# A four-layer graph transformer on one core: two bias rows fetched later, expert offsets in fp16, column sums on ScalarE, half a Gram matrix

## What is computed

```python
# layer 0 mixer, twice: ... h = gelu(y @ W1 + b1); stream += h @ W2 + b2
# layer 0 experts (8, two chosen per node):
combine = chosen_weights                        # 1250 x 8
x = x + sum_e combine[:, e] * (relu(y @ w1[e] + b1[e]) @ w2[e] + b2[e]) + shared
# layer 3 mixer:
XW_v, theta_X = X @ W_v.T, X @ W_theta.T
first = mean(XW_v, axis=nodes)                  # = mean(X) @ W_v.T
kv = theta_X.T @ XW_v                           # = W_theta (X.T X) W_v.T
x = x + first + X @ kv / (n * sqrt(d))
```

## Time and profile before

| | |
|---|---|
| median of 3 runs | 3285.67 us (3276.35 to 3289.95) |
| profiled execution | 3295.35 us, of which the span is 3293.6 us |
| busy, share of the span | PE 85%, DVE 51%, POOL 36%, ACT 32% |
| mean granted clock of PE | 0.91 |
| DMA | 415.33 MB, mean 126 GB/s |

### The profile page before, as it was taken

The page is one execution under the profiler, slowest core; times in us unless marked ns, Lnnn a source line. Parts: engine busy times, 40 slices in busy tenths (PEclk is TensorE's granted clock), DMA queues, the critical chain, the costliest instruction groups (busy, mean ns, idle before and its releaser), DMA issues. The chain is left out here.

```text
span 3293.6 us, 45745 instructions
## 1 busy us (share of the span) xinstructions
PE 2804.8 (85%) x16779; PEld 1790.3 (54%) x16779; DVE 1675.3 (51%) x3399; ACT 1067.9 (32%) x2432; POOL 1182.0 (36%) x1445
## 2 busy tenths in 40 slices
PE   8997899869999986989997893999879968669874
PEld 4654567535556754555554562777535646445553
DVE  8765667523556762266643536222245456552543
ACT  3243436312432642122321431444332315320132
POOL 2031677638367763863312122111103306400042
PEclk9998989889998988998998896999989979888887
DMA  2001445324144531451100001999820039710098
GB/s 61 1 26 58 124 148 163 103 67 128 36 119 143 159 118 48 128 138 34 41 19 26 13 26 53 412 417 416 332 53 30 33 114 325 244 42 0 32 342 270
DMA packets 163939, 415.33 MB, mean 126 GB/s; under 512 B 23931, under 2 KB 75675, under 8 KB 140236
## 3 DMA queue, kind: packets, MB, share of 16 engines
q1 hardware_dynamic: 149213, 362.10, 32.4%
q0 software_dynamic: 12960, 42.48, 3.4%
q10 hardware_dynamic: 1555, 7.95, 1.0%
HBM read 325.37 MB, written 87.09 MB: 125 GB/s over the span
## 5 line engine op out<-in xcount | busy, mean ns | idle before, releaser
L2587 POOL TENSOR_SCALAR raw<-raw 128x512 f32<-128x512 f32 x380 | 261.9, 689 | 1219.9 <-PE ps L492 300.8
L506 PE MATMUL ps<-units,ARENA 128*125 128x512 f16 x2160 | 479.2, 384 | 56.8 <-POOL units L2591 56.2
L506 PEld LDWEIGHTS ps<-units,ARENA 128*125 128x125 f16 x2160 | 292.8, 138 | 238.7 <-POOL units L2591 56.8
L1751 DVE TENSOR_TENSOR ARENA<-tmp,ARENA 128x500 f16<-128x500 f32 (+3 forms) x289 | 198.4, 690 | 399.2 <-ACT ARENA L1326 215.9
L492 PE MATMUL ps<-ARENA,units 128*128 128x500 f16 (+1 forms) x2160 | 389.0, 342 | 2.0 <-DVE ARENA L2476 2.0
L492 PEld LDWEIGHTS ps<-ARENA,units 128*128 128x128 f16 x2160 | 211.5, 98 | 179.3 <-issue 7.8
L1325 ACT ACTIVATE tmp<-ps,cols 128x500 f32<-128x500 f32 (+1 forms) x204 | 129.7, 636 | 443.1 <-PE ps L492 402.4
L2591 POOL TENSOR_TENSOR AT<-raw,AT 128x512 f16<-128x512 f32 x200 | 235.9, 1179 | 17.0
L2591 POOL TENSOR_TENSOR units<-raw,units 128x512 f16<-128x512 f32 x180 | 220.0, 1222 | 15.3
L2635 POOL DMA_INDIRECT ARENA<-rows_d,proj x81 | 80.3, 991 | 389.0 <-DVE ARENA L2106 363.0
L2640 POOL DMA_INDIRECT picks_d<-ARENA,proj x81 | 81.9, 1011 | 347.4 <-DVE ARENA L2146 346.7
(11 more groups left out here) (439 smaller groups left out, 4856.7 us busy)
## 6 DMA issues: line engine op xcount, KB each, us to landing
ARENA<-split_d SPq DMA_DIRECT2D x135, 1024.0 KB
raw<-in_moe SPq DMA_DIRECT2D x200, 256.0 KB, 3.0
split_d<-AT SPq DMA_DIRECT2D x200, 256.0 KB, 2.5
raw<-in_units SPq DMA_DIRECT2D x180, 256.0 KB, 2.5
ARENA<-split_d SPq DMA_DIRECT2D x27, 1280.0 KB
rows_d<-ARENA SPq DMA_DIRECT2D x6, 896.0 KB
ARENA<-picks_d SPq DMA_DIRECT2D x6, 896.0 KB
ARENA<-picks_d ACTq DMA_DIRECT2D x6, 896.0 KB
```

What stands on the lines that cost most here:

```text
L506: ins = pe.matmul(o[0:R, :], th(srcT, h, k, t, 1), w(k, g), start=(i == 0), stop=(i == len(steps) - 1))
L1751: tt(lo, tmp[:, staged[0] % STAGES, 0:width], hi, ALU.subtract).then_inc(sem("lo_T"), s.one("lo_T"))
L2587: pool.tensor_scalar(r, r, WEIGHT_SCALE, 1.0, ALU.mult, ALU.mult).then_inc(sem("pool_step"), 1)
```

## The change

It has four parts. The note of the place for b20 and b21 is taken in block 1 of the MLP, with its second unit, instead of block 0 with its first. The expert offsets are one fp16 product on 72 rows: rows 0 to 7 hold the high part of the combination weights with the high part of the biases, rows 32 to 39 the weights' low part with the high part, rows 64 to 71 the high part with the biases' low part; the rest is zero. DVE prepares the biases (`bias_parts`, between the low parts) and the weights (in `gates`), and E0's slot is freed there. The column sums of layer 3 come from the accumulator output of ACT's evictions of M's transposes, and DVE adds the three chunks. Of the Gram matrix PE computes for block k only the columns from 128 k on; the blocks below the diagonal are transposed from those above (`gram_below`), and ACT evicts them to their places.

```diff
@@ -198,7 +198,10 @@
-        combT = K[0:NE, N:2 * N]
+        combT = K[0:72, N:N + N // 2].bitcast(F16)
+        comb_parts = K[0:R, 2000:2000 + T * 72].rearrange("p (t e) -> p t e", e=72)
+        comb_hi = K[0:R, 2720:2720 + T * NE // 2].bitcast(F16).rearrange("p (t e) -> p t e", e=NE)
+        bias_rows16 = K[0:72, 2800:2800 + D // 2].bitcast(F16)
         comb3 = comb[0:R, :].rearrange("p (t e) -> p t e", e=NE)
@@ -237,6 +240,7 @@
+        column_sums = stats[:, :, 0:1].rearrange("p (k c) a -> p k (c a)", k=KC)
@@ -780,7 +784,6 @@
                     if b == 0:
-                        uses_row()
                         by_chunks(lambda c: transposed_chunk(lambda t, a, b: nat(Y, t, a, b), "y", "yT", c),
@@ -788,6 +791,8 @@
                     u, w = unit()
+                    if b == 1:
+                        uses_row()
                     gemm_N("Q", lambda k, g: w[:, g, k, :], "read_dve", by_chunk=True, waits=(0, KC, KC) if b == 0 else (KC, KC, KC))
@@ -847,14 +852,13 @@
                     for j in range(nt):
-                        ins = pe.transpose(o[0:8, j * R:(j + 1) * R], comb3[:, t0 + j, :], ident[0:R, 0:R])
+                        ins = pe.transpose(o[0:72, j * R:(j + 1) * R], comb_parts[:, t0 + j, :], ident[0:R, 0:R])
                     ins.then_inc(sem("filled_act"), 1)
                 pe.wait_ge(sem("combT"), s.more("combT", 3))
-                pe.wait_ge(sem(f"row_loaded{ROWS.index(row) % ROW_SLOTS}"), 16 * (ROWS.index(row) // ROW_SLOTS + 1))
                 for t in range(T):
...
                     o = bank("dve", "read_dve")
-                    pe.matmul(o[0:R, :], combT[:, t * R:(t + 1) * R], row_slots[0:8, ROWS.index(row) % ROW_SLOTS, :], start=True, stop=True).then_inc(sem("filled_dve"), 1)
+                    pe.matmul(o[0:R, :], combT[:, t * R:(t + 1) * R], bias_rows16, start=True, stop=True).then_inc(sem("filled_dve"), 1)
@@ -1247,19 +1251,29 @@
-            for k in range(KC):
+            def gram_rows(k):
                 pe.wait_ge(*left("act"))
...
                 for t in range(T):
-                    ins = pe.matmul(o[:, :], nat(M, t, k * 128, (k + 1) * 128), nat(M, t), start=(t == 0), stop=(t == T - 1))
+                    ins = pe.matmul(o[:, k * 128:D], nat(M, t, k * 128, (k + 1) * 128), nat(M, t, k * 128, D), start=(t == 0), stop=(t == T - 1))
                 ins.then_inc(sem("filled_act"), 1)
-            pe.wait_ge(*left("dve"))
-            o = bank("dve", "read_dve")
-            for k in range(KC):
-                for t in range(T):
-                    ins = pe.matmul(o[:, k:k + 1], nat(M, t, k * 128, (k + 1) * 128), ones[0:R, 0:1], start=(t == 0), stop=(t == T - 1))
-            ins.then_inc(sem("filled_dve"), 1)
-            pe.wait_ge(sem("G"), s.more("G", KC))
+
+            def gram_below(k):
+                pe.wait_ge(sem("G"), s.more("G", 2 if k == 2 else 1))
+                pe.wait_ge(*left("act"))
+                o = bank("act", "G")
+                for j in range(k + 1, KC):
+                    ins = pe.transpose(o[:, j * 128:(j + 1) * 128], G[:, k * D + j * 128:k * D + (j + 1) * 128], ident[:, :])
+                ins.then_inc(sem("filled_act"), 1)
+
+            gram_rows(0)
+            gram_rows(1)
+            gram_below(0)
+            gram_rows(2)
+            gram_below(1)
+            gram_rows(3)
+            gram_below(2)
+            pe.wait_ge(sem("G"), s.more("G", KC - 1))
             pe.wait_ge(*loaded(True))
@@ -1327,13 +1341,14 @@
-            def evac_direct(dst, order="c", groups=None):
+            def evac_direct(dst, order="c", groups=None, sums=None):
...
                     direct_banks.append(o)
-                    act.activation(th(dst, 0, k, t0, nt), o[:, 0:nt * R], ACT.Identity).then_inc(sem("hi_D"), s.one("hi_D"))
+                    act.activation(th(dst, 0, k, t0, nt), o[:, 0:nt * R], ACT.Identity,
+                                   accum_out=sums(k, t0 // CH[0][1]) if sums else None).then_inc(sem("hi_D"), s.one("hi_D"))
@@ -1576,7 +1591,7 @@
                 for t0, nt in CH:
-                    evac("act", "combT", combT[:, t0 * R:(t0 + nt) * R], nt * R, p=8)
+                    evac("act", "combT", combT[:, t0 * R:(t0 + nt) * R], nt * R, p=72)
@@ -1688,10 +1703,26 @@
-            by_chunks(lambda c: evac_direct("YT", groups=(KC * c, KC * c + KC)), high_chunk)
+            by_chunks(lambda c: evac_direct("YT", groups=(KC * c, KC * c + KC), sums=lambda k, c: column_sums[:, k, c:c + 1]), high_chunk)
             evac("both", "x_sel", x_sel[0], D, p=SEL)
-            for k in range(KC):
-                evac("act", "G", G[:, k * D:(k + 1) * D], D)
+            def gram_rows(k):
+                act.wait_ge(sem("filled_act"), s.more("filled_act"))
+                o = s.bank("act")
+                act.activation(G[:, k * D + k * 128:(k + 1) * D], o[:, k * 128:D], ACT.Identity).then_inc(sem("G"), s.one("G"))
+
+            def gram_below(k):
+                act.wait_ge(sem("filled_act"), s.more("filled_act"))
+                o = s.bank("act")
+                act.activation(G[:, (k + 1) * D:].rearrange("p (j c) -> p j c", c=D)[:, :, k * 128:(k + 1) * 128],
+                               o[:, (k + 1) * 128:D].rearrange("p (j c) -> p j c", c=128), ACT.Identity).then_inc(sem("G"), s.one("G"))
+
+            gram_rows(0)
+            gram_rows(1)
+            gram_below(0)
+            gram_rows(2)
+            gram_below(1)
+            gram_rows(3)
+            gram_below(2)
             for k in range(KC):
@@ -2287,8 +2318,26 @@
                     step(tt(w1, w1, lg, ALU.mult))
-                    step(tt(comb3, w1, bc(mr), ALU.mult), "comb")
-                    step(ts(combs[0:R, :], comb[0:R, :], WS, None, ALU.mult))
+                    step(tt(comb3, w1, bc(mr), ALU.mult))
+                    ts(combs[0:R, :], comb[0:R, :], WS, None, ALU.mult)
+                    step(dve.tensor_copy(comb_hi, comb3))
+                    dve.tensor_copy(comb_parts[:, :, 0:8], comb_hi)
+                    dve.tensor_copy(comb_parts[:, :, 64:72], comb_hi)
+                    step(tt(comb_parts[:, :, 32:40], comb3, comb_hi, ALU.subtract), "comb")
+
+            def bias_parts(name):
+
+                j = ROWS.index(name)
+                dve.wait_ge(sem(f"row_loaded{j % ROW_SLOTS}"), 16 * (j // ROW_SLOTS + 1))
+                slot = row_slots[0:72, j % ROW_SLOTS, :]
+                dve.memset(comb_parts, 0.0)
+                ts(slot, slot, WEIGHT_SCALE, None, ALU.mult).then_inc(sem("dve_step"), s.one("dve_step"))
+                dve.wait_ge(*s.latest())
+                dve.tensor_copy(bias_rows16, slot).then_inc(sem("dve_step"), s.one("dve_step"))
+                dve.wait_ge(*s.latest())
+                tt(bias_rows16[64:72, :], slot[64:72, :], bias_rows16[64:72, :], ALU.subtract).then_inc(sem("dve_step"), s.one("dve_step"))
+                dve.wait_ge(*s.latest())
+                row_free(name)
@@ -2300,12 +2349,12 @@
             low_parts("Q", "hT", 0)
+            bias_parts("E0")
             low_direct("YT", (8, 12))
...
             low_parts("Q", "hT", 2)
-            add_to(X, "read_dve", scale=1.0)
-            row_free("E0")
+            add_to(X, "read_dve")
             for e in range(NE):
@@ -2515,9 +2564,9 @@
-            dve.wait_ge(sem("filled_dve"), s.more("filled_dve"))
-            o = s.bank("dve")
-            ts(colsT[:, 0:4], o[:, 0:4], 1.0 / N, None, ALU.mult).then_inc(sem("read_dve"), s.one("read_dve"))
+            dve.tensor_reduce(colsT[:, 4:8], column_sums, AX_X, ALU.add).then_inc(sem("dve_step"), s.one("dve_step"))
+            dve.wait_ge(*s.latest())
+            ts(colsT[:, 0:4], colsT[:, 4:8], 1.0 / N, None, ALU.mult).then_inc(sem("dve_step"), s.one("dve_step"))
             dve.wait_ge(*s.latest())
@@ -2700,7 +2749,7 @@
                 if name[0] == "E":
-                    sp.dma_start(slot[0:40, :], eb_in[int(name[1])]).then_inc(sem(f"row_loaded{j % ROW_SLOTS}"), 16)
+                    sp.dma_start(slot[0:72, :], eb_in[int(name[1])]).then_inc(sem(f"row_loaded{j % ROW_SLOTS}"), 16)
                 elif name == "gb2":
@@ -2877,9 +2926,9 @@
     rows = np.stack([r[n] for n in VEC_ROWS])
-    eb = np.zeros((4, 40, D), np.float32)
+    eb = np.zeros((4, 72, D), np.float32)
     for i, rows_of in enumerate((a["L0_ffn_b2"], a["L1_ffn_be2"], np.concatenate([a["L2_ffn_n1"], a["L2_ffn_n2"]], 1), a["L3_ffn_b2"])):
-        eb[i, 0:NE] = eb[i, 32:32 + NE] = rows_of
+        eb[i, 0:NE] = eb[i, 32:32 + NE] = eb[i, 64:64 + NE] = rows_of
     proj = a["L0_mix_proj"].transpose(0, 2, 1)
```

## The result

| | kernel before | changed kernel |
|---|---|---|
| median | 3281.01 us (4 runs, 3273.92 to 3289.95) | 3197.10 us (4 runs, 3192.38 to 3201.46) |
| profiled execution | 3295.35 us, span 3293.6 | 3192.38 us, span 3190.6 |
| mean granted clock | 0.910 | 0.926 |

The ratio is 0.9743, with a 95% interval of 0.9711 to 0.9774: 84 us, where 96 were forecast. The two profiled executions lie 103 us apart. Neither number is the gain: the profiled execution of before took longer than each of its four runs, that of after is the fastest of its own, and the experiments show what they differ in besides the change. In one later series one execution (offsets_early_again, 3426.54 us at a granted clock of 0.825) was in a slower state of the chip, and its median is given without it.

What follows compares the result with a forecast made beforehand. TensorE was taken as the bound, with time lost to its idle gaps, extra work and low clock. Terms 60.6 + 8.0 + 25.7 + 2.2 - 0.4 = 96.1 us, taken from 3285.67, gave 3190 us, range 3172 to 3222.

Steps and rivals of the forecast that it cites:

- The row's place: Second MLP block's W2, layer 0: later bias row load removes 56.2 us idle and 4.3 us low clock, together 60.6 us.
- to spare: Second block's W2: POOL has its weights split at 686, PE wants them at 701.0, leaving 15 us.
- The offsets: Layer 0's expert bias product: faster products less DVE's added work win 8 us, bounds 6.6 to 10.5.
- The ten products: Experts' offset matmuls: paced by DVE's evictions, they take 5.7 us where L857 holds PE 16.36 us.
- DVE's four instructions: Between hT's low parts and the last direct low parts: 2.35 us, 2.45 with waits, all on the path.
- Column sums and Gram matrix: Layer 3: the stretch falls from 49.35 to 23.6 us, 25.7 won; the W_v product behind it wins 2.2.
- The end wait: Before the product with W_v: the last two evictions follow each other on ACT, about 1.1 us, bounds 0.6 and 1.6.
- the accumulator's reads: ACT's twelve evictions of layer 3's transposes: 211 ns each, 0.4 us lost, bounds 0 and 2.5.
- POOL as the bound in block 2: Rival, second MLP block: DVE's row addition slows POOL, PE stands 30 us in all, 3220 us; chance 0.07.
- The queue standing: Rival: SP's queue also waits at the row's new place, 28 us lost twice, 3250 us; chance 0.03.
- The clock down in the Gram stretch: Rival, layer 3: clock stays low from 384 columns on, 7.4 us become 15, 2.2 stay lost, 3200 us; chance 0.09.
- Slower by a late E0 row: Rival, experts: DVE waits for E0's row, each us late costing one; above 3302 needs 112 us; chance 0.01.

Runs made afterwards that it cites:

- offsets_early_again: Second series of the changed kernel with DVE's four new instructions one call earlier, before the low parts of hT's first chunk; 3198.97 us against the changed kernel's 3192.43.
- the run with one unit: Kernel before with only the bias row's load one unit later instead of three; 3233.35 us, ratio 0.9836 to the kernel before.
- offsets_early: Changed kernel with DVE's four new instructions one call earlier, before the low parts of hT's first chunk; first series 3189.48 us against the changed kernel's 3204.39.
- three_memsets: Changed kernel with three more DVE memsets of 600 columns between its memset and the scaling of E0's row; 3202.05 us in one run.

## Why the prediction was right, and where not

- **The total.** Forecast 96.1 us. The changed kernel was compared with the one before three times: 83.9, 92.4 and 101.2 us by the medians, 92.5 in the mean (the ratios, 0.9743, 0.9728 and 0.9703, stand for 84, 90 and 98). The forecast of 3190 us lies 7 under the first median; the range 3172 to 3222 held it. The timelines give 60.9 + 6.6 + 28.6 = 96.1 us, the very sum that was forecast. That is luck in the last digit: the terms were off by +0.3, -1.4 and +1.1 us, which cancel.
- **The row's place**, 60.6: measured 60.9 in the timeline. Both halves (56.2 of idle time, 4.3 of low clock behind it) went whole: no gap is left, and W2 takes 26.06 us both times. The chain from DVE's tenth addition over SP and POOL to PE was the right one, as the run with one unit shows. POOL had 12.8 us to spare, not 15.
- **The offsets**, 8: this is the step that was mis-sized; the runs have 6.6. The ten products came as forecast (5.49 for 5.7), DVE's four instructions too (2.15 for 2.45, up to 3.27 beside GpSimd). But the 16.36 us that they replace was read from one execution, and the mean over six is 15.2: 1.1 us less. I costed DVE's delay as its own length, where PE's wait grew by 1.9 to 3.4 us (2.6 in the mean) depending on what GpSimd did to DVE at that moment. And a term was missing: the 48 gate products behind that wait took 5.1 us in each of the five traces with the new offsets in the old order, all at the low clock, and 3.2 to 5.1, mean 4.3, in the six with the old ones. The W2 behind the offsets gave back 0.7 us (28.9 to 28.2), and some 0.5 lie in smaller pieces.
- **Column sums and Gram matrix**, 25.7 + 2.2 for the stretch: measured 28.6. The end wait was 0.42 us (forecast 1.1), and the accumulator's reads of 0.19 to 0.21 us, for which 0.4 was taken off, cost next to nothing: PE's last wait in the transposes ahead is 1.68 us where it was 1.58.
- **The rivals.** POOL as the bound in block 2: no gap, though its instructions were longer as the rival said, by 2 us over the unit where the rival had 15. The queue standing: 1.2 us once. The clock down in the Gram stretch: 1.00. (Its price was too low as written: "384 columns and fewer" takes in gram_rows(1), another 6.5 us, so 3206 and not 3200.) The Trainium skill (TensorE: Matmul & The Clock Gate, "Part 4: PE-mode transpose") says that the full clock doesn't engage for transposes. For the six between the blocks that does not hold: they ran at a clock of 1.00 and did not lower it. But they are 0.8 us among 22 us of matmuls, so what a long stretch of transposes alone does to the clock is not shown here. Slower by a late E0 row: DVE did not wait for it, not even 17 us earlier (offsets_early). That a late row costs 1:1 was shown for DVE's own time alone (three_memsets).
- **What was missing.** Nothing in the prediction said that an execution of either kernel carries up to two stretches of 10 us whose clock is chance. The 13.6 us by which the runs of before spread was the hint, and it was used for the range only. It also makes the separate gains by medians (70.5 + 8.7 + 26.6 = 105.8) and the whole (92.5) disagree, while those of the timelines add up.

## What to carry to other kernels

A load that sits in a shared queue ahead of its slot's release holds up all that is behind it; what it costs is the time at which the next weights are ready less the time at which they are wanted, and the wait of the queue can be far longer than that. Tiny matmuls can cost more than their own time: behind the 80 of one column the next product took 16.14 us instead of 14.00, so taking them off TensorE won twice. Weigh a change of 10 us by the same stretch in several timelines, never by two medians, and place new DVE work where DVE waits for another engine, not where another engine waits for it.

## What was not expected of the hardware

The clock was low while TensorE had no gap. It fell over the 80 matmuls of one column, behind Gram products at full clock. And in 8 of 14 executions it was low over the last context products, of 65 fp32 columns, in the second attention (12.05 us for 56 instead of 6.36), in 9 of 14 in the first; in the execution shown PE had waited 0.25 us just ahead of that gapless row, and the clock was low from its start. Both in the kernel before, its second attention and its column sums:

```profile
1012.00:1030.00 18.00, 18.00 (x84) 17.65 (x85) 3.25 (x4) 0.00 (x0) 13.19 (x17) 0.50 0.49 147
```

```profile
3027.00:3042.00 15.00, 15.00 (x82) 15.00 (x81) 0.07 (x1) 0.60 (x1) 0.00 (x0) 0.57 0.00 0
```

PE is busy for the whole of both stretches, at a clock of 0.50 and 0.57: a full row in the profile does not say that the clock is up. And a DVE cast of 0.42 us took 1.25 beside a GpSimd subtraction, while a memset at the same place kept its 0.66.
